# First cross attention of a perceiver: the next pair's maximum moved ahead of the last low part of a slot on VectorE

## The reference, cut to what matters

```python
x = x + _L0_xattn_ref(_layernorm(x), ctx_512, ctx_512, Wq, bq, Wk, bk, Wv, bv, Wo, bo)
# x: 16 x 64 x 512, ctx_512: 16 x 1601 x 256, 16 heads of 32
qh = (q @ Wq + bq) in heads;  kh = (k @ Wk + bk) in heads;  vh = (v @ Wv + bv) in heads
scores = einsum('bhqd,bhkd->bhqk', qh, kh) / sqrt(32)
attn = softmax(scores, axis=-1)
out = einsum('bhqk,bhkd->bhqd', attn, vh)
return out (heads joined) @ Wo + bo
```

## Time and profile before

| | before |
|---|---|
| median of 3 runs | 1854.89 us (1854.12 to 1860.37) |
| profiled execution | 1855.92 us, span 1854.2 us |
| busy, share of the span | TensorE 87%, VectorE 62%, ScalarE 49%, GpSimd 43% |
| granted TensorE clock over the span | 0.945 of full |
| granted clock from 100 to 800 us (changed stage) | 1.00 |
| first maximum, last maximum of the stage | 108.6 us, 879.9 us |
| scores of batch 1 to scores of batch 15 | 155.46 to 838.89 us, 14 batches of 48.8 us |

### The profile page before, as it was taken

How to read it: one execution, slowest core, us unless ns; L and a number is a source line. 1 busy time by engine, 2 the same in 40 slices (tenths; PEclk the granted TensorE clock), 3 DMA queues, 4 the chain that set the end, 5 groups by cost and what they waited for, 6 DMA issues and landing times. The chain is left out here.

```text
span 1854.2 us, 34146 instructions
## 1 busy us (share of the span) xinstructions
PE 1614.7 (87%) x13913; PEld 830.4 (45%) x14024; DVE 1156.2 (62%) x1983; ACT 908.5 (49%) x1261; POOL 802.5 (43%) x402
## 2 busy tenths in 40 slices
PE   4799999999999999995789999899789989699449
PEld 2345555555555555553345464345334443344114
DVE  4477788787887887874355467789422221726881
ACT  1267777777777777776163133411112221227750
POOL 2258777787777777775106614522000000003410
PEclk9899999999999999996789979999899999799769
DMA  2459999999999999997325551233738943000001
GB/s 111 121 123 179 189 185 185 185 186 189 190 183 184 184 183 187 189 172 144 93 64 188 176 213 52 70 124 125 309 122 332 398 178 134 0 1 1 0 1 46
DMA packets 517543, 273.31 MB, mean 147 GB/s; under 512 B 443776, under 2 KB 495488, under 8 KB 514320
## 3 DMA queue, kind: packets, MB, share of 16 engines
q1 hardware_dynamic: 517392, 271.18, 60.5%
HBM read 138.74 MB, written 22.54 MB: 87 GB/s over the span
## 5 line engine op out<-in xcount | busy, mean ns | idle before, releaser
L516 POOL TENSOR_TENSOR x<-x_prob,x 128x1604 bf16<-128x1604 f32 x128 | 413.2, 3228 | 189.3 <-ACT x L647 175.7
L629 ACT ACTIVATE x_prob<-x_score,x_negmax 128x1604 f32<-128x1604 f32 x128 | 204.5, 1597 | 100.3 <-DVE x_negmax L740 100.2
L540 PE MATMUL x_ring<-x_ctx_hi,wk_split 128*128 128x400 bf16 (+1 forms) x1024 | 219.0, 336 | 26.3 <-DVE x_kT L704 16.9
L740 DVE TENSOR_REDUCE x_negmax<-x_score 128x1 f32<-128x1604 f32 x128 | 231.6, 1809 | 8.3 <-PE x_score L557 8.3
L704 DVE SCALAR_TENSOR_TENSOR x_kT<-x_ring,bk,x_kT 128x400 bf16<-128x400 f32 (+1 forms) x256 | 162.3, 634 | 108.0 <-ACT x_kT L618 105.9
L540 PE MATMUL x_ring<-wv_split,x_ctx_hi 128*128 128x512 bf16 (+1 forms) x770 | 200.3, 379 | 9.6 <-issue 9.5
L647 ACT CAST x<-x_prob 128x1604 bf16<-128x1604 f32 x128 | 195.9, 1531 | 0.3
L710 DVE TENSOR_TENSOR x_v<-x_ring,x_v 128x512 bf16<-128x512 f32 (+1 forms) x208 | 143.1, 688 | 39.2 <-ACT x_v L622 32.2
L618 ACT ACTIVATE x_kT<-x_ring,bk 128x400 bf16<-128x400 f32 (+1 forms) x196 | 116.6, 595 | 78.4 <-PE x_ring L540 76.9
L573 PE MATMUL x_pv<-x_pT,x_v 128*64 128x128 bf16 (+1 forms) x3328 | 123.7, 227 | 27.0 <-DMA x_pT<-x 15.8
L540 PEld LDWEIGHTS x_ring<-x_ctx_hi,wk_split 128*128 128x128 bf16 x1024 | 89.7, 97 | 126.1 <-DVE x_kT L704 38.0
(11 more groups left out here) (317 smaller groups left out, 2540.3 us busy)
## 6 DMA issues: line engine op xcount, KB each, us to landing
y_ctx<-in_ctx SPq DMA_DIRECT2D x16, 1664.0 KB, 10.4
y_ctxT<-in_ctxT SPq DMA_DIRECT2D x16, 1601.0 KB, 14.0
x_stage<-in_ctxT SPq DMA_DIRECT2D x48, 400.0 KB, 4.5
x_q_rows<-q_rows SPq DMA_DIRECT2D x64, 128.0 KB, 3.3
m_xT<-in_L_ffn_w SPq DMA_DIRECT2D x16, 512.0 KB, 4.8
ffn_w_parts<-m_xT SPq DMA_DIRECT2D x32, 256.0 KB, 2.7
x_stage<-in_ctxT SPq DMA_DIRECT2D x16, 401.0 KB, 5.1
x_pT<-x SPq DMA_TRANSPOSE x256, 4.3
```

The source lines that it names most:

```text
L516: pool.tensor_tensor(ph[:, g % 2, 1, 0:NKP], prob[:, g % 2, :], ph[:, g % 2, 0, 0:NKP], ALU.subtract).then_inc(pl_done, 1)
L540: last = pe.matmul(out_, lhs, rhs, start=(i == 0), stop=(i == len(steps) - 1))
L629: nc.scalar.activation(prob[:, g % 2, :].rearrange("p (c n) -> p c n", n=QW), scores, ACT.Exp, bias=nmax[:, g % 2:g % 2 + 1], accum_out=rs ...
L740: dve.tensor_reduce(nmax[:, pair % 2:pair % 2 + 1], scores, mybir.AxisListType.XY, ALU.max, negate=True).then_inc(max_done, 1)
```

## The change

On VectorE, the last low part of a slot is not written at the end of the slot but kept in a list, `held`. It is written in the next slot, directly behind that slot's maximum and ahead of the sum. "Last" is by ring number: in slot 2 of batches 1 to 15 the last ring number is the output's, so nothing is held there. Slot 7 holds nothing either (`p < NPAIR - 1`). Nothing else is moved; the reciprocal of the slot now stands ahead of the held part.

```diff
@@ -728,6 +728,7 @@
             split_chunk(0, 1)
+            held = []
             for n in range(NPROJ):
@@ -739,13 +740,19 @@
                         dve.wait_ge(s_done, pair + 1)
                         dve.tensor_reduce(nmax[:, pair % 2:pair % 2 + 1], scores, mybir.AxisListType.XY, ALU.max,
                                           negate=True).then_inc(max_done, 1)
+                    while held:
+                        project_lo(*held.pop())
                     if 3 <= pair:
                         summed(pair - 3)
+                    last = [g for e, g, _ in ring_events(b, p) if g is not None][-1:]
                     for e, g, vector in ring_events(b, p):
                         if e[0] == "proj":
                             if vector:
                                 project_hi(e[1], 1 - b % 2, g)
-                            project_lo(e[1], 1 - b % 2, g)
+                            if g in last and p < NPAIR - 1:
+                                held.append((e[1], 1 - b % 2, g))
+                            else:
+                                project_lo(e[1], 1 - b % 2, g)
```

## The result

The changed kernel takes 1847.51 us (median of 7 runs, 1846.06 to 1851.01) against 1854.89 us (7 runs): a ratio of 0.996, 95% interval 0.9947 to 0.9972. The forecast was 1847.1 us. The profiled execution took 1848.18 us, its span is 1846.5 us for 1854.2.

What follows compares the result with a forecast made beforehand. TensorE's work plus its waits, mainly 15.5 us for VectorE's low parts of key groups, set the pace. Batches 1 to 14 give -6.7 us, batch 0 -1.1, total -7.8: 1847.1 us from 1854.89, range 1843 to 1853.5 (own spread 1843.5 to 1850).

Steps and rivals of the forecast that it cites:

- (a): VectorE's maximum waits for the scores alone and starts 0.79 us after T, the start of a slot's scores.
- delay d: Lateness of the maximum beyond T+0.79; slots 1, 5, 7 lose d each, slots 2, 4, 6 lose d - 0.04.
- rivals 1 and 2: Late maximum delays the held bank: gain cancelled, 1854 to 1855 us (chance 0.17), or slower, 1860 or more (0.05).
- (b): Next slot's third group waits for the held bank, free at T+3.21 (key part) or T+3.27 (value part).
- Slot 5's loss: Slot 5's third group waits for slot 4's held V part: 6.28 us for 5.71, +0.57.
- rival 3: No new stall in slot 5: -1.05 us a batch and 1839 us; chance 0.02.
- (c): TensorE's fourth group: bank free by T+3.95 to 4.01, wanted at 4.24 or later, so its wait is gone.
- Slot 3: Maximum behind slot 2's output comes at T+1.02 for T+1.65; bank free 3.63, wanted 3.72; 5.71 us for 6.22.
- Batch 0: Slots 1 and 2 gain 2.0 us, slot 3 loses 0.57, slots 4 to 7 lose 0.39; together -1.1 us.
- The sum: Slot gains and losses in batches 1 to 14: -0.48 us a batch, -6.7 us over 14.
- Rival 4, the port rule: Held key low parts on VectorE stand behind GpSimd operations reading SBUF; 14 us added, 1861 us; chance 0.02.
- Rival 5, transfers: Transfers set the pace, so the time stays at 1854 to 1855 us; chance 0.04.

Runs made afterwards that it cites:

- Sum first: Changed kernel with the held low part one place later, behind maximum and sum; 1863.16 us, ratio 1.0042 to the kernel before.
- slot 1 held: Changed kernel's hold limited to slot 1; 1847.29 us, ratio 0.9961 to the kernel before.
- values held: Changed kernel's hold limited to value slots 4 and 6 (and slot 2 of batch 0); 1866.81 us, ratio 1.0055 to the kernel before.
- the kernel with the exchange in slot 0: Against the changed kernel: holds only in slots 1, 3, 5; in slot 0 ScalarE writes the fourth high part before the conversion; 1831.01 us.

## Why the prediction was right

- *(a) The maximum at T+0.79.* It is 0.78 to 0.79 in slots 1, 2, 4, 5, 6 and 7 of all batches 1 to 14, so the delay d of rivals 1 and 2 is 0.00, though here another group follows the scores. Sum first, which adds 0.20 to the bank's release, shows that both rivals had their slope right: it costs 1.12 a batch (1.08 expected) and the kernel turns slower.
- *(b) The held bank.* T+3.21 and 3.27 forecast, 3.22 and 3.27 measured. Slot 5's loss was forecast at 0.57 and measured at 0.55; the two runs that hold keys only and values only turn it off and on. That refutes rival 3 as well.
- *(c) No wait at the fourth group*: right, and none for the sum.
- *Slot 3.* The chain over the output came out to 0.01 us (high part 4.80, maximum at 1.02). The slot took 5.67, not 5.71: I had taken slot 5 as free of waits, and it carries 0.04. One step rests on less than it seems: "about 4.8" takes ScalarE's reader 0.16 us behind the start of the products that follow the group, as measured here (460.20 behind 460.04), but the only such distance worked out ahead was (a)'s 0.25. With 0.25 the high part comes at 4.89 and slot 3's margin of about 0.08 is gone.
- *Batch 0.* -1.1 forecast, -1.10 measured.
- *The sum.* Per batch -0.48 forecast, -0.54 measured (-7.79 over 14, for -6.7). The 0.04 of slot 3, some hundredths in slots 1 and 5, and 0.4 us of waits for transposes that the kernel before had and this one has not make most of the difference.
- *The total agrees better than the parts, and that is luck.* The stage gained 1.1 us more than forecast and the first scores came 0.45 early by scatter; 1.64 us, for which the forecast had no term, were given back behind the stage. 0.63 of these are in the first seven slots of batch 15 (40.29 us for 39.66). Its slot 1 runs at a granted clock of 0.50 (0.62 before), the lower level of 1.2 GHz, and takes 4.91 us for 4.39; TensorE was busy for 1.63 of the 4.80 us of slot 0 ahead of it in both kernels; its slot 3 gives the same 0.52 back, with the scores at full clock there (4.40 us for 4.92). Its slot 4 takes 0.51 more because the products wait longer for a transpose (start at T+4.55 for 4.04), and slot 2 takes 0.12 more. The other 1.01 are later and are not assigned to a cause. The windows of slot 1, after and before, then the products of slot 4, after and before (scores at 853.94 and 863.16):

```profile
834.35:839.26 4.91, 2.75 (x50) 1.75 (x50) 2.19 (x4) 3.22 (x4) 3.23 (x1) 0.50 0.87 163
...
843.69:848.08 4.39, 2.24 (x50) 1.64 (x50) 2.19 (x4) 3.21 (x4) 2.81 (x1) 0.62 0.88 165
...
858.49 1.60 PE L573 MATMUL x_pv<-x_pT,x_v 128*64 128x128 bf16 x26 [3.32 <-DMA x_pT<-x]
...
867.20 1.60 PE L573 MATMUL x_pv<-x_pT,x_v 128*64 128x128 bf16 x26 [2.81 <-DMA x_pT<-x]
```

- *The range.* Its parts, 1.3, 1.1 and 0.7 us around 1847.1, give 1844.0 to 1850.2, not 1843.5 to 1850.
- *Rival 4, the port rule* (the Trainium skill, SBUF — State Buffer). After the change the 224 key low parts of batches 1 to 14 ran 623 to 641 ns, as before it. The 84 held ones of these batches, key and value, all start 1.74 or 1.75 us after the maximum's start, though a GpSimd operation overlaps each of them. The rule as I read it, with a bias pointer as an input, does not hold for this operation.
- *Rival 5, transfers*: no wait for a transpose stood in the changed kernel's batches 1 to 14. They came with shorter batches and later conversions, in the runs above.

## What to carry to other kernels

Moving an operation past another moves everything that it releases: write down who waits for the moved one (here a ring bank, wanted by the third group of the next slot) and price it for each shape of slot, because the same move gained 0.37 us in slot 1, behind a key slot, and lost 0.55 in slot 5, behind a value slot. Apply it only where the operation in front is really late; a sixth of the moves gave more than all of them. Then look for what made it late: exchanging two steps in another engine's order, in every slot but one, gave 1831.16 us for the move's 1847.51, but an order counted by places has to be looked at slot by slot, since the same place held something else in slot 2.

## What the runs showed of the hardware

- The stages behind the change are the same in all kernels, yet from batch 15's first scores to the end the profiled executions took 1014.5 (slot 1 held) to 1021.3 us (values held). The +6.0 of the values-held kernel goes with a lower granted clock there (0.94 for 1.00 in the windows shown). Of the changed kernel's +1.64, batch 15 shows both signs of the clock, +0.52 and -0.52, and 0.51 of a wait for a transpose. What decides when the clock falls was not tried.
- A mean DMA share near or above 1 was no sign of a bound. It is 1.02 in slot 1 before, and the kernel with the exchange in slot 0 runs its batches 1.6 us faster in the mean, with 1.24 in slot 6 of batch 7, and waits 1.2 us for transposes in all of batches 1 to 14.
